# First attention's softmax factors spread by DMA through DRAM; second attention's maxima products as 64-row pairs, its head quads in the score banks' rotation

## The reference, cut to what matters

```
x = x + tanh(g_xattn[0]) * L0_xattn(layernorm(x), ctx)    # first attention: 32 heads of 128, 8 kv heads,
      # keys = context and latents (768 a batch); rms-normalised q and k; softmax(q k^T / sqrt(128)) v; @ Wo
x = x + tanh(g_ffn[0])   * L0_ffn(layernorm(x))           # relu^2 ffn with a small expert path, layernorm
x = x + tanh(g_xattn[1]) * L1_xattn(layernorm(x), ctx)    # second attention: 32 heads of 16, 8 kv heads, 512 keys
      # softmax(q k^T / 4) v; @ Wo
x = x + tanh(g_ffn[1])   * L1_ffn(layernorm(x))           # dynamically quantised SwiGLU
```

## Time and profile before

| | us |
|---|---|
| median of 3 runs (1023.63 to 1025.63) | 1024.17 |
| the profiled execution | 1025.66 |
| its span | 1023.8 |
| PE busy | 982.4 (96%) |
| DVE busy | 628.1 (61%) |
| ACT busy | 501.9 (49%) |
| POOL busy | 356.8 (35%) |

### The profile page before, as it was taken

How to read it: one execution, slowest core, us unless ns; L and a number is a source line. 1 busy time by engine, 2 the same in 40 slices (tenths; PEclk the granted TensorE clock), 3 DMA queues, 4 the chain that set the end, 5 groups by cost and what they waited for, 6 DMA issues and landing times. The chain is left out here.

```text
span 1023.8 us, 18226 instructions
## 1 busy us (share of the span) xinstructions
PE 982.4 (96%) x6748; PEld 846.9 (83%) x6748; DVE 628.1 (61%) x1102; ACT 501.9 (49%) x969; POOL 356.8 (35%) x244
## 2 busy tenths in 40 slices
PE   4999999999999999999999999999999999999996
PEld 3879989998998899899989989898977776666655
DVE  5567457556745754675566467556653865777746
ACT  4356337534743663464366346435624413656534
POOL 3335316233531623344163334423333530440033
PEclk9989999999999999999999999999999997999999
DMA  6011002001100210020011002000034207722001
GB/s 225 1 62 43 2 1 102 1 0 34 68 0 0 64 39 0 3 99 0 0 61 41 0 0 102 20 0 1 2 96 149 96 16 184 175 40 47 2 1 42
DMA packets 31460, 46.53 MB, mean 45 GB/s; under 512 B 3520, under 2 KB 15424, under 8 KB 31424
## 3 DMA queue, kind: packets, MB, share of 16 engines
q1 hardware_dynamic: 30848, 46.03, 15.1%
q10 hardware_dynamic: 576, 0.00, 0.0%
HBM read 41.83 MB, written 4.19 MB: 45 GB/s over the span
## 5 line engine op out<-in xcount | busy, mean ns | idle before, releaser
L438 DVE TENSOR_TENSOR ptL<-tbank,ptH 128x512 fp32r<-128x512 f32 x192 | 132.2, 688 | 82.9 <-ACT ptH L298 82.7
L298 ACT ACTIVATE ptH<-tbank 128x512 fp32r<-128x512 f32 x192 | 115.8, 603 | 91.2 <-PE tbank L550 90.6
L550 PE MATMUL tbank<-ident,probs 128*128 128x128 f32 x864 | 131.1, 276 | 5.3 <-DVE qTL L440 2.8
L324 ACT ACTIVATE probs<-score,negmax 128x768 f32<-128x768 f32 x128 | 115.7, 904 | 29.6 <-DVE negmax L451 29.6
L451 DVE TENSOR_REDUCE negmax<-score 128x1 f32<-128x768 f32 x128 | 118.8, 948 | 14.4 <-PE score L80 14.4
L78 PE MATMUL obank<-ptH,vH 128*128 128x256 f32 x384 | 121.4, 316 | 0.0
L409 DVE TENSOR_REDUCE sumsq<-probs 128x2 f32<-128x256 f32 (+1 forms) x80 | 42.1, 526 | 113.3 <-ACT probs L293 71.8
L550 PEld LDWEIGHTS tbank<-ident,probs 128*128 128x128 f32 x864 | 97.9, 140 | 14.5 <-DVE probs L417 3.0
L206 POOL TENSOR_TENSOR rnorm<-sumsq,neg_half 128x2 f32<-128x2 f32 (+1 forms) x80 | 72.0, 902 | 107.5 <-DVE sumsq L411 107.4
L80 PE MATMUL score<-wkvH,kvT_lo 128*128 128x256 f32 x384 | 108.7, 283 | 0.0
L79 PE MATMUL score<-wkvL,kvT_hi 128*128 128x256 f32 x384 | 108.7, 283 | 0.0
(11 more groups left out here) (272 smaller groups left out, 2301.8 us busy)
## 6 DMA issues: line engine op xcount, KB each, us to landing
wqo_stage<-in_wq SPq DMA_DIRECT2D x9, 1024.0 KB, 5.6
wqo_stage<-in_wo SPq DMA_DIRECT2D x8, 1024.0 KB, 5.1
wkv_stage<-in_wkv SPq DMA_DIRECT2D x9, 512.0 KB, 6.4
a_qS<-q_scratch SPq DMA_DIRECT2D x24, 128.0 KB, 4.9
ctx_stage<-in_ctxT SPq DMA_DIRECT2D x2, 1024.0 KB, 13.5
kS<-k_scratch SPq DMA_DIRECT2D x32, 64.0 KB, 3.2
q_scratch<-qpart SPq DMA_DIRECT2D x16, 128.0 KB, 1.9
wqo_stage<-in_down_w SPq DMA_DIRECT2D x3, 512.0 KB, 3.5
```

Of the source, the lines that this page charges most:

```text
L298: act.activation(out, tbank[c % 2][:], ACT.Copy, scale=scale).then_inc(t_hi, 1)
L324: act.activation(probs[:, m % NP, :], score[m % 2][:, 0:SKV], ACT.Exp, bias=negmax[:, m:m + 1], accum_out=rsum[:, m:m + 1]).then_inc(s_exp, 1)
L438: i = dve.tensor_tensor(out, tbank[c % 2][:], f32(hi), ALU.subtract)
L550: i = pe.transpose(tbank[c % 2][:, n * P:(n + 1) * P], block_in, S.ident[:])
```

## The change

First attention: factors no longer go through TensorE and ScalarE. SP writes the four columns of reciprocals of a head to a DRAM row and reads it back spread over the partitions into a buffer `factors`. `normalise_o` reads that, writes `o_norm`, and itself waits for `o_lo_part` of the head before. Reciprocals move ahead of the unit's second maximum. In unit 0, score tile 2 and its maximum move ahead of chunk 0.

```diff
@@ attn0
     for u in range(U):
         if u % 2 == 0 and u // 2 + 1 < GRP:
             order.append(("q", u // 2 + 1))
-        if u % 2 == 1 and u >= 3:
-            order.append(("r", (u - 3) // 2))
         order += [("p", CH * u + j) for j in range(CH)]
-    order.append(("r", GRP - 1))
@@ sync
                 S.load_wkv(sp, g + 1)
+                for h in range(GRP):
+                    spread_factors(g, h)
+
+            def spread_factors(g, h):
+                sp.wait_ge(r_inv, GRP * g + h + 1)
+                for n in range(RT):
+                    sp.dma_start(r_dram[h, n * P:(n + 1) * P].rearrange("(q a) -> q a", a=1),
+                                 rsum[:, 4 * h + n:4 * h + n + 1]).then_inc(r_out, 16)
+                sp.wait_ge(r_out, 16 * RT * (GRP * g + h + 1))
+                sp.dma_start(factors[:], r_dram[h].partition_broadcast(P)).then_inc(r_in, 16)
             def last():
                 S.load_wo(sp, LAST)
+                for h in range(GRP):
+                    spread_factors(LAST, h)
...
@@ scalar: `factors` is gone, and its three calls
             def hi_o(g, h):
-                act.wait_ge(t_lo, TC * g + at["r", h] + 1)
+                act.wait_ge(o_normed, GRP * g + h + 1)
@@ vector
             def normalise_o(g, h):
-                c = at["r", h]
-                dve.wait_ge(t_hi, TC * g + c + 1)
+                dve.wait_ge(r_in, 16 * (GRP * g + h + 1))
                 dve.wait_ge(pe_pv, 24 * g + 2 * CH * (h + 1))
-                dve.tensor_tensor(o_norm[:], obank[h % 2][:], o_norm[:], ALU.mult).then_inc(t_lo, 1)
+                if h:
+                    dve.wait_ge(o_lo, GRP * g + h)
+                dve.tensor_tensor(o_norm[:], obank[h % 2][:], factors[:], ALU.mult).then_inc(o_normed, 1)
...
                         lo_q(g, 1)
-                        lo(g, ("p", 0), ptL[:, 0, :], ptH[:, 0, :])
                     if u + 1 < U:
                         maximum(g, 2 * u + 2)
+                    if u == 0:
+                        lo(g, ("p", 0), ptL[:, 0, :], ptH[:, 0, :])
...
                         normalise_o(g, (u - 3) // 2)
+                    if u % 2 == 1:
+                        reciprocals(g, u // 2)
                     if u + 1 < U:
                         maximum(g, 2 * u + 3)
...
-                    if u % 2 == 1:
-                        reciprocals(g, u // 2)
@@ tensor: `transpose_factors` is gone, and its three calls; times_v waits for o_normed
                     if u == 0:
+                        scores(g, 1, (0,))
                         transpose_probs(g, 0, 0)
-                    if u + 1 < U:
+                        scores(g, 1, (1,))
+                    elif u + 1 < U:
                         scores(g, u + 1)
```

```diff
@@ attn1, tensor
+        def add_maxima(m, h, own):
+            if own:
+                pe.wait_ge(s_max, 4 * m + 4)
+            else:
+                pe.wait_ge(pe_own, 2 * m + h + 1)
             for t in range(2):
-                for s in range(2):
-                    c = (4 * m + 2 * t + s) % 16
-                    x = pe.matmul(scoreT[h][:, 512 * s:512 * (s + 1)].rearrange("p (k q) -> p k q", k=2)[:, :, t * P:(t + 1) * P],
-                                  negmax[:, c:c + 1].to_broadcast([P, P]),
-                                  S.ident_r[:].unsqueeze(1).to_broadcast([P, 2, P]), start=False, stop=t == 1)
-            x.then_inc(pe_sT, 1)
+                for r, rows in enumerate(half_rows):
+                    s = r if own else 1 - r
+                    c, q = (4 * m + 2 * t + s) % 16, t * P + r * P // 2
+                    x = pe.matmul(scoreT[h][:, 512 * s:512 * (s + 1)].rearrange("p (k q) -> p k q", k=2)[:, :, q:q + P // 2],
+                                  negmax[rows, c:c + 1].to_broadcast([P // 2, P]),
+                                  S.ident_r[rows, r * P // 2:(r + 1) * P // 2].unsqueeze(1).to_broadcast([P // 2, 2, P // 2]),
+                                  start=False, stop=t == 1 and not own)
+            x.then_inc(pe_own if own else pe_sT, 1)
...
         for m in range(NM):
             if m + 1 < NM:
                 scores(m + 1, 0)
-            scores_T(m, 0)
-            if m >= 2:
-                times_v((m - 2) // 2, m % 2)
+            for h in range(2):
+                scores_T(m, h)
+            for own in (True, False):
+                for h in range(2):
+                    add_maxima(m, h, own)
             if m + 1 < NM:
                 scores(m + 1, 1)
+            if m % 2 == 0 and m >= 4:
+                transpose_o((m - 4) // 2)
...
-            scores_T(m, 1)
-            if m % 2 == 1 and m >= 3:
-                transpose_o((m - 3) // 2)
+            if m >= 2:
+                times_v((m - 2) // 2, m % 2)
```

More of the change, by code:

```diff
@@ L117, in attn0 @@
     oTH, oTL = sb("oTH", [P, GRP, ROWS], f32r), sb("oTL", [P, GRP, ROWS], f32r)
-    o_norm = sb("o_norm", [P, ROWS], fp32)
+    o_norm, factors = sb("o_norm", [P, ROWS], fp32), sb("factors", [P, ROWS], fp32)
+    r_dram = nc.dram_tensor("r_scratch", (GRP, ROWS), fp32, kind="Internal").ap()
+    r_out, r_in, o_normed = sem("r_out"), sem("r_in"), sem("o_normed")
     ss, rn = sb("sumsq", [P, 40], fp32), sb("rnorm", [P, 40], fp32)
@@ L560, in transpose_q, with scores @@
                 transposes(g, ("q", h), [q_rows[:, t, h * D0:(h + 1) * D0] for t in range(RT)])
[L562 to L566, removed]
+            def scores(g, u, tiles=(0, 1)):
                 h, b = u // 2, u % 2
@@ L1279, in transpose_q @@
             for i in range(2):
-                if t == 1:
+                if t == 1 and i == 0:
+                    pe.wait_ge(free.o_step, 2 * free.heads)
+                if t == 1 and i == 1:
                     pe.wait_ge(free.x_add, 1)
@@ L1360, in attn1, with score_bank @@
     half_rows = [slice(0, P // 2), slice(P // 2, P)]
+    users = [("s", e) for e in range(4)]
+    for m in range(NM - 1):
+        users += [("s", 4 * (m + 1) + e) for e in range(4)]
+        if m % 2 == 0 and m >= 4:
+            users.append(("o", (m - 4) // 2))
+    place = {user: n for n, user in enumerate(users)}
+    def score_bank(kind, n):
+        return score[place[kind, n] % NB if (kind, n) in place else NB - 1]
     def unit(m):
@@ L1431, in scalar @@
             exp(m, 1)
+        copy_o(NW - 2)
         copy_oT(1)
@@ L1443, in windows, with maxima @@
                 dve.tensor_copy(vcol[:, i % 2, s, :, 0:D1], v_rows[:, :, g * D1:(g + 1) * D1]).then_inc(win, 1)
-        def maxima(m):
-            for e in range(4 * m, 4 * m + 4):
+        def maxima(m, t):
+            for e in range(4 * m + 2 * t, 4 * m + 2 * t + 2):
                 dve.wait_ge(pe_s, e + 1)
-                dve.tensor_reduce(negmax[:, e % 16:e % 16 + 1], score[e % NB][:], AX.X, ALU.max,
+                dve.tensor_reduce(negmax[:, e % 16:e % 16 + 1], score_bank("s", e)[:], AX.X, ALU.max,
                                   negate=True).then_inc(s_max, 1)
@@ L1461, in finish @@
                               o_inv[:, w % 2].unsqueeze(3).to_broadcast([P, 2, GRP, D1]), ALU.mult).then_inc(o_step, 1)
-        maxima(0)
+        for t in range(2):
+            maxima(0, t)
         dve.wait_ge(ones_set, 1)
@@ L1465, in vector @@
         for m in range(NM):
+            if m + 1 < NM:
+                for t in range(2):
+                    maxima(m + 1, t)
             if m % 2 == 0 and m >= 4:
                 finish((m - 4) // 2)
-            if m + 1 < NM:
-                maxima(m + 1)
             if m % NV == 1 and m // NV + 1 < TURNS:
@@ L1482, in tensor, with wait_free @@
     def tensor(pe):
+        def wait_free(kind, n):
+            at = place[kind, n]
+            if at >= NB:
+                kind, n = users[at - NB]
+                if kind == "s":
+                    pe.wait_ge(s_max, n + 1)
+                else:
+                    pe.wait_ge(o_step, 2 * n + 2)
         def scores(m, t):
@@ L1537, in transpose_o @@
         def transpose_o(w):
+            if w < NW - 2:
+                wait_free("o", w)
+            else:
+                pe.wait_ge(o_step, 2 * w)
             pe.wait_ge(o_copied, w + 1)
             for t in range(2):
-                x = pe.transpose(obank[:, SQ + t * P:SQ + (t + 1) * P], o_quad[:, w % 2, t * P:(t + 1) * P], S.ident[:])
+                x = pe.transpose(score_bank("o", w)[:, t * P:(t + 1) * P], o_quad[:, w % 2, t * P:(t + 1) * P], S.ident[:])
             x.then_inc(pe_oT, 1)
```

48 lines of the change are left out of this document (19 added, 29 removed).

## The result

| | before | after |
|---|---|---|
| median, us | 1024.90 (1023.63 to 1025.94, 4 runs) | 1123.03 (1117.63 to 1126.10, 4 runs) |
| profiled execution, its span | 1025.66, 1023.8 | 1122.17, 1120.3 |
| first attention ends (first ffn product) | 755.7 | 863.0 |
| first ffn | 95.4 | 95.4 |
| second attention's units, first scores to last | 121.8 | 111.2 |

The ratio is 1.095 (95% interval 1.091 to 1.100): 98 us slower, where 11 faster was forecast. The four stretches say where: first attention costs 107 more, second attention 10.6 less. The forecast for the second was 12.0 and for the first +0.5.

What follows compares the result with a forecast made beforehand. TensorE, busy 982.4 of 1023.8 us, was taken as the bound. First attention -19.3 + 13.3 + 3.5 + 3 = +0.5, second attention -12.0: 1024.17 + 0.5 - 12.0 = 1012.7, said as 1013 us; range 998 to 1034.

Steps and rivals of the forecast that it cites:

- the price of the element transfers: First attention, reciprocals written to DRAM: landing 0.9 us behind the weights at head 0 (0.3 to 4.1), 1.9 elsewhere.
- Heads 1 to 3, "hidden": First attention's turns: the factor chain of about 6 us fits in about 11.6 us between reciprocals and use; no cost.
- Head 0: First attention: factors queue behind weight loads; VectorE waits 2.0 us, 1.9 reach TensorE in seven turns, +13.3 us.
- The last turn: First attention's end: second attention's weights queue behind the spreading; TensorE idles 3.5 us before head 2's output products.
- The clock: After the last turn's idle, one stretch of 6.8 us at half clock costs 3 us; none counted in other turns.
- Rival (b): First attention: head 0's waits drop the clock each turn (1037), or element transfers are slow (1040); together chance 0.25.
- Factor groups, -14.1: First attention: 32 groups of factor transposes go, 0.44 us each, all on TensorE's path; 14.1 us saved.
- tbank, -2.4: First attention, turn's end: transposes no longer wait for a tbank held by a factor group; 8 x 0.3 us saved.
- Unit 0's order, -2.8: First attention, turn's start: earlier score tile 2 and maximum shorten the wait for an exponential; 0.35 us a turn saved.
- Second attention, -12.0: Second attention: 64-row pairs for the maxima cut two units from 7.52 to 6.77 us; 16 times, 12.0 us saved.
- Its bound of 17: Second attention: the most that could be saved, 17 us, if only TensorE's work counts.
- The pair's price: Second attention: a pair of 64-row products of the maxima takes 0.115 us, eight pairs a unit 0.92.

Runs made afterwards that it cites:

- e9: The changed kernel with only the first of a head's four element transfers, the spread reading a row of x: 1080.58 us, ratio 1.055.
- e11: The changed kernel with single elements written to DRAM 512 B apart, the spread reading a row of x: 1027.56 us, ratio 1.004.
- e3: The changed kernel with one transfer of 128 pieces of 16 B replacing four of 4 B pieces, read with a stride: 1027.79 us, ratio 1.003.
- e6: e3 with head 0's spreading ahead of the next wq and wkv loads, and second attention's weights ahead of the last turn's spreading: 998.75 us, ratio 0.974.
- e4: The changed kernel with element transfers written to SBUF instead of DRAM, the spread reading a row of x: 1030.63 us, ratio 1.006.
- e12: e6 with unit 0 of a turn in the order of the kernel before the change: 1004.81 us, ratio 0.981.
- e1: First attention as before the change, second attention as after it: 1014.26 us, ratio 0.989.
- e7: e1 with second attention's maxima added by 128-row products, in the new place: 1019.39 us, ratio 0.996.
- e10: The changed kernel with each of a head's four transfers writing 128 pieces of 16 B, the spread reading a row of x: 1029.95 us, ratio 1.006.
- e8: e1 with a maxima group's four 64-row products issued two and two by row half instead of alternating: 1011.10 us, ratio 0.986.

## Why the prediction was wrong

- **The step that failed** is the price of the element transfers: "the four element transfers land behind that: at least 0.3 later; at most 4.1", 0.9 taken at head 0 and 1.9 elsewhere. They took about 7 us (235.4 us of SP in 32 waits), 7.3 for a single transfer in e9. The upper bound came from a 4.1 us landing of another kind: a read of 128 elements from DRAM. No row of the trace before held a write of single elements, and the bound was taken as if one did.
- **What that step cost, and what it did not**: in e11 the same four transfers land in order (1.5 us) and the kernel takes 1027.56, so 95 of the 110 us between 1013 and 1123 are this step's (e3, which leaves nothing out, gives the same). The other 15 are the sizes below. With a landing near the forecast's the time would have been inside the range, but no gain.
- **Heads 1 to 3, "hidden"**: their chain was given 6 us and 5.6 to spare. With 9.0 to the spread and 4.4 for its landing (2.4 forecast) it is 13.4 and sticks out of 11.04 (head 2: of the 9.6 that it has in e3 and e6); TensorE idled 2.9 to 4.0 us at head 2 in every turn. Had the landing been the row's 1.9, the step would have held: in e3, `o_norm` of head 1 stands 11.0 to 12.6 behind the reciprocals and that of head 2 9.6, with no wait; at head 3 of the seven turns VectorE waits up to 1.4, which TensorE does not feel, as forecast.
- **Head 0**: place and mechanism right, 1.9 us forecast. With the landing in order (e3) it is 2.5, so +17.5 for +13.3; in the change it was 6.6 to 8.0. In e3 the spreading transfer of head 0 landed after 3.0 to 3.4 us and not after 2.4, and VectorE waited 2.2 on average (2.0 forecast); TensorE lost a little more than that and not, as forecast, a little less.
- **The last turn**: the chain right, 3.5 us forecast, 4.8 with the landing in order, 10.3 in the change.
- **The clock**: 3 us for one stretch; 31.6 in products. Rival (b) named both causes of its own, the fallen clock (+24) and slow elements (+27), but as two separate ways to about 1040. They came together and fed each other: a longer wait in every turn is also a longer stretch at 1.2 GHz, and two heads a turn waited, not one. That is how 1123 lies 83 us above it. In e3 and e4 waits of 1.9 to 3.1 us did bring the clock down in 12 of 14 turns, so (b)'s first half was right as well; but for 3.4 us each, which costs 1.7 and not the 3.4 that (b) took. e3's products take 8.9 us more than e6's (682.9 to 674.0).
- **Factor groups, -14.1, and tbank, -2.4**: together 8 x (90.92 - 89.51) = 11.3 (e12). The 32 groups do go. Laid side by side, product by product, a turn of before and one of e12 show where the rest went. The groups of heads 0 and 1 save some 0.4 each, and 4.9 us behind each of them the transposes that now wait 0.23 for `ptL` take the same 0.4 back, in every turn. The groups of heads 2 and 3 keep theirs, and the tbank step falls from 0.43 to 0.12, as forecast. What failed is "all on TensorE's path": for half of the groups the low half of a chunk on VectorE was the next limit, right behind.
- **Unit 0's order, -2.8**: 8 x (89.51 - 88.97) = 4.3 by the turns. The medians of e12 and e6 stand 6.1 apart; part of that is ahead of the turns. So the gross gain was 15.6, not 19.3; e6's first attention ends 15.5 earlier than before.
- **Second attention, -12.0**: -10.5 (e1). Period 6.72 for 6.77, which would be 16 x 0.80 = 12.8; the difference is at the head, where the second and third two units take 11.0 and 7.6 us in the change for 10.1 and 7.5 before, and which the forecast took at zero, give or take 2. Its bound of 17 does not follow from its own terms: 7.52 - 3.07 - 3.5 is 0.95, and 16 of them are 15. The pair's price was right (0.115; 0.112 by the starts in e1's trace), but it is no less than a 128-row product's: those start 0.115 us apart in e7's trace. What the pairs save is the change between 128 and 64 rows, which e7 shows as a longer step at three places: 0.21 ahead of the products, 0.22 behind the first, 0.21 after the last. From the last transposed scores to the next scores e7 takes 1.35 us on average, e1 1.05: 0.30 a unit, half of the 0.59.
- *The Trainium skill*, "DMA: Bandwidth & Descriptors", section "Specifications", says that below 512 B a read-modify-write is done. It was cited beside (b) as something no run showed. The runs now agree in part: 4 B side by side are slow (7.3 us), but 4 B at 512 B from each other (1.5) and 16 B side by side (1.5 to 2.2) are not. What the rule would do here deserved a chance and a time among the rivals, not a note beside one.

The result lies 89 us above the range's end. Head 0, heads 1 to 3 and the last turn all rest on the same landing, so their errors were one error, and its bound was a row of another kind.

## What to carry to other kernels

Don't let a loop wait for single 4 B elements written side by side to DRAM: write 16 B a partition and let the reader take the stride, and issue a short chain ahead of bulk loads in its queue. When a change puts a transfer of a shape the trace has never held on a path that recurs, price the case in which it is too long for its cover at every place, with the fallen clock on top, before adding up the rest. When work is taken out of the busiest engine's queue, ask how far behind the next limit stands: here half of the groups that went gave nothing.

## What the runs showed of the hardware that was not expected

- A transfer of 128 pieces of 4 B to neighbouring addresses in DRAM was confirmed after 7.3 us (e9), to addresses 512 B apart after 1.5 (e11), of 16 B side by side after 1.5 (e3) or 2.2 (e10), and of 4 B to SBUF after 1.8 (e4). For most of the 7 us the DMA engines stood idle. SP took about 0.44 us for one more such issue (four in 1.74).
- After most idles of 1.9 to 4.1 us in a turn the clock stood at 1.2 GHz for 3.4 or 6.8 us, after two of 7.9 and 8.0 for 10.2. The length of the idle alone does not decide it: none followed 3.35 us at 320.8 in the change, and one followed 1.85 at 81.7 in e3. In e6, whose turns have no idle over 1 us, none occurred from 59 to 740 us.
- Second attention's start at 1.2 GHz varies from one profiled execution to another: 13.7 us (before, e6, e12), 17.1 (after, e8), 20.5 (e1), none (e3, e7). It goes with the spread within a kernel's runs: e1 took 1008.5 us at a mean clock of 0.996 and 1019.5 at 0.984. What decides it stays open.
